# One matrix product of a delta-rule loop is moved behind two others in the order of the matrix engine

## What is computed

```python
def step(St, inp):
    q_i, k_i, u_i, kcd_i, dec_i, g_i = inp
    attn = jnp.einsum('bhid,bhjd->bhij', q_i, k_i) * dec_i
    v_new = u_i - jnp.einsum('bhid,bhdv->bhiv', kcd_i, St)
    inter = jnp.einsum('bhid,bhdv->bhiv', q_i * jnp.exp(g_i)[..., None], St)
    out_i = inter + jnp.einsum('bhij,bhjv->bhiv', attn, v_new)
    g_last = g_i[..., -1]
    St_new = St * jnp.exp(g_last)[..., None, None] + jnp.einsum('bhid,bhiv->bhdv', k_i * jnp.exp(g_last[..., None] - g_i)[..., None], v_new)
    return (St_new, out_i)
```

## Time and profile before

| | |
|---|---|
| median of 3 runs | 3433.17 us |
| lowest, highest | 3423.48, 3434.26 us |
| the profiled execution's own time | 3425.84 us |
| its span, first to last instruction | 3424.1 us |
| PE busy | 3096.7 us (90%) |
| PE's weight loads busy | 2439.5 us (71%) |
| DVE, ACT, POOL busy | 69%, 57%, 55% |
| mean granted clock of TensorE | 0.936 |

### The profile page before, as it was taken

The page is one execution under the profiler, slowest core; times in us unless marked ns, Lnnn a source line. Parts: engine busy times, 40 slices in busy tenths (PEclk is TensorE's granted clock), DMA queues, the critical chain, the costliest instruction groups (busy, mean ns, idle before and its releaser), DMA issues. The chain is left out here.

```text
span 3424.1 us, 150774 instructions
## 1 busy us (share of the span) xinstructions
PE 3096.7 (90%) x57344; PEld 2439.5 (71%) x57344; DVE 2362.8 (69%) x5828; ACT 1954.4 (57%) x5384; POOL 1866.6 (55%) x3982
## 2 busy tenths in 40 slices
PE   3599999999999999999999999999999999945880
PEld 2477777777777777777777777777777777722660
DVE  2377777777777777777777777777777777775114
ACT  2366666666666666666666666666666666630000
POOL 1265555555555555555555555555555555522773
PEclk8699999999999999999999999999999999976555
DMA  9201010111000000101111011010101010103555
GB/s 120 51 19 28 17 31 18 28 21 28 21 25 20 28 21 25 25 25 23 22 24 24 25 18 31 18 28 16 31 18 31 18 31 18 31 1 84 131 116 127
DMA packets 113784, 121.25 MB, mean 35 GB/s; under 512 B 17140, under 2 KB 105684, under 8 KB 113236
## 3 DMA queue, kind: packets, MB, share of 16 engines
q1 hardware_dynamic: 107608, 113.78, 15.2%
q0 software_dynamic: 6144, 7.09, 1.4%
HBM read 103.00 MB, written 17.01 MB: 35 GB/s over the span
## 5 line engine op out<-in xcount | busy, mean ns | idle before, releaser
L863 DVE SCALAR_TENSOR_TENSOR conv<-raw,conv_w,conv 128x256 f32<-128x256 f32 x1560 | 775.8, 504 | 447.4 <-ACT conv L741 410.3
L1096 POOL TENSOR_TENSOR core_ms<-core_ss,q_scale 128x2 f32<-128x2 f32 x256 | 74.9, 293 | 1028.8 <-ACT squares L794 1028.8
L498 PE MATMUL bank<-xT,w_proj 128*128 (+1 forms) x2080 | 564.9, 395 | 43.6 <-DMA w_proj<-in_w_proj 43.6
L781 ACT COPY rounds<-pair_bank 128x768 f32<-128x768 f32 x516 | 409.5, 794 | 245.8 <-PE pair_bank L577 245.8
L915 DVE TENSOR_TENSOR plus_one<-rounds,ident_half 128x256 f32<-128x256 f32 x774 | 411.0, 531 | 196.9 <-ACT rounds L781 186.7
L577 PE MATMUL pair_bank<-rounds 64*64 64x64 f32 x18576 | 457.4, 225 | 3.0 <-ACT rounds L781 3.0
L577 PEld LDWEIGHTS pair_bank<-rounds 64*64 64x64 f32 x18576 | 371.2, 134 | 111.3 <-issue 111.3
L498 PEld LDWEIGHTS bank<-xT,w_proj 128*128 128x128 f32 x2080 | 356.9, 191 | 103.1 <-issue 66.1
L768 ACT ACTIVATE vb<-bank,v_scale 128x128 f32<-128x128 f32 x516 | 162.1, 370 | 439.6 <-PE bank L529 439.6
L577 PE MATMUL pair_bank<-rounds,plus_one 64*64 64x64 f32 x10320 | 282.9, 221 | 23.0 <-DVE plus_one L915 5.3
L648 PE MATMUL bank<-w_out,gated 128*128 128x256 f32 x1024 | 285.7, 401 | 8.8
(11 more groups left out here) (275 smaller groups left out, 6598.7 us busy)
## 6 DMA issues: line engine op xcount, KB each, us to landing
e_blk<-e_rows SPq DMA_DIRECT2D x260, 128.0 KB, 4.0
g_blk<-g_rows SPq DMA_DIRECT2D x262, 64.0 KB, 3.4
w_gate_up<-in_w_gate_up SPq DMA_DIRECT2D x64, 192.0 KB, 2.8
w_proj<-in_w_proj SPq DMA_DIRECT2D x17, 512.0 KB, 4.0
table<-zeros_wide SPq DMA_DIRECT2D x32, 262.0 KB, 9.5
part<-table SPq DMA_DIRECT2D x32, 256.0 KB, 9.7
w_down<-in_w_down SPq DMA_DIRECT2D x16, 384.0 KB, 5.4
w_z<-in_w_proj SPq DMA_DIRECT2D x17, 256.0 KB, 3.1
```

Of the source, the lines that this page charges most:

```text
L498: mm = te.matmul(bank[bk][:, place * 2 * BLK:(place + 1) * 2 * BLK], w, k.xT[:, kt, bass.ds(rr * 2, 2)].rearrange("p c b i -> p b c i"), s ...
L781: a.copy(rounds[:, i % 2].rearrange("p b s w x -> p b (s w x)"), pair_bank[:, :, 0:6 * C]).then_inc(s["ul_out"], 1)
L863: v.scalar_tensor_tensor(out=conv[:, t], in0=raw[:, t, :, w:w + BLK], scalar=conv_w[:, t, w:w + 1], in1=conv[:, t], op0=ALU.mult, op1=ALU. ...
```

## The change

`project_out(st, n)` goes from ahead of `grow(st + 1, ...)` to behind `sum_squares(n + 2)`. Nothing is added or left out, and the orders of the other engines stay.

```diff
                 attend(st + 1, n, slot + 1)
                 a_round(m, 5)
-                project_out(st, n)
                 grow(st + 1, n, slot + 1)
                 sum_squares(n + 2)
+                project_out(st, n)
                 project(rr1, Z_ + 1, 0, 1, "projected_z")
                 turn_core(st + 1, m)
                 a_round(m, 6)
```

## The result

The changed kernel takes 3497.49 us (median of 4 runs, 3488.66 to 3498.46) against 3432.28 us before (4 runs, 3423.48 to 3434.26). The ratio is 1.0189, with a 95% interval of 1.0165 to 1.0214. So it is slower by 65 us; 59 were forecast.

A forecast was written before the change was run, and what follows sets the result against it. PE's order was taken to bound the loop. A stall of 0.68 us at the sums of squares, net 0.46 a body over 128 bodies, adds 59 us to 3429.2: forecast 3488 us, range 3466 to 3516.

The forecast's parts named there:

- The delay at the release: At the sums of squares: time from the end of ACT's square until PE goes on, taken as 0.12 us.
- step 5: Gate's projection on PE: behind the output projection instead of quarter-array work it is 0.10 us shorter, 0.87 for 0.97.
- 0.04 behind such an end: On DVE: `add_y` starts 0.04 us behind the output projection's modelled end, at 1504.44.
- what the queue swallows: At the transposes' weight load on PE: a possible 0.06 us lateness from `add_y`, taken as 0.
- the 0.46 of the sum: End of each body: `turn_core` at 1505.11 against 1504.65, 0.46 us later; 128 bodies give 59 us.
- Rival 2: On DVE: `add_one` still takes 1.00 us, making a body 0.83 longer, +106 us, 3535 us; chance 0.05.
- Rival 1: At the sums of squares: the square isn't late, PE needn't stand still, 28 us gained, 3401 us; chance 0.07.
- the 28 us: On PE: without any wait `turn_core` starts 0.22 us earlier in each body, 28 us in all.
- The lower bound of the range: No delay at the release: 0.34 us a body, +44 us, counted from the lowest run, 3467 us.

The follow-up runs named there:

- its control: The kernel before, with the sums of squares taken of the same constant tile so PE has no wait for ACT's square: 3428.86 us, ratio 0.9989.

## Why the prediction was right, point by point

**The mechanism** is the one forecast. The sums of squares were covered by the output projection; without that cover PE stands and waits for ACT. The wait is 0.66 in the timeline (0.68 forecast), it grows to 1.19 with the sums still earlier, and the loss goes with it in two kernels that remove it by different means.

**The terms**, on the clock of the earlier trace rows: growth 0.32 behind round 5's last part (0.36), sums at 1502.25 (1502.24), output projection at 1503.28 (1503.27), gate's projection at 1504.25 (1504.24). The delay at the release was bounded by 0 and 0.24 and taken as 0.12; it is 0.13, 1509.64 to 1509.77. The gate's projection is 1.03 long, not 1.13, as step 5 had it.

**The term that was mis-sized** is the start of `add_y`, "0.04 behind such an end". By the rows above, the projection's modelled end is 1510.80 + 1.13 = 1511.93 and `add_y` starts at 1512.12, so 0.19 behind. Less 7.52, it ends at 1505.02 (1504.86 forecast), and the weights of the transposes load at 1505.13:

```profile
1512.65 0.20 PEld L641 LDWEIGHTS bank<-ident,core_n 128*128 128x128 f32 x2 [0.26 <-issue]
```

That is 0.21 behind where they would have loaded unhindered (1504.92), past what the queue swallows: the transposes are 0.05 late, the gate 0.08 (1505.61 for 1505.53), and with that the body shown. Over the 128 bodies the mean is 0.50 more than before, for the 0.46 of the sum: 64 us for 59.

No run took this delay away by itself, but the trace of the changed kernel has bodies without it. In six blocks of each pair of heads `add_y` takes the place of its sum from a loop's counter; in the last two, which stand behind that loop in the code, the place is a constant. In these 32 bodies `add_y` starts 0.04 behind the projection's modelled end, in the other 96 it starts 0.16 to 0.18 behind (0.19 by the rounded rows above). One of the 32, on PE and DVE:

```profile
1577.73 1.10 PE L511 MATMUL bank<-ones_col,sq 128*64 128x1 f32 x32 [0.66 <-ACT sq L751]
1578.76 1.13 PE L648 MATMUL bank<-w_out,gated 128*128 128x256 f32 x4
...
1580.59 0.38 PE L641 MATMUL bank<-ident,core_n 128*128 128x128 f32 x2
```

```profile
1579.93 0.42 DVE L951 TENSOR_TENSOR y_sum<-bank,y_sum 128x256 f32<-128x256 f32 x1 [0.76 <-PE bank L648]
```

The transposes start 2.86 behind the sums (2.87 forecast, 1502.24 to 1505.11), and these bodies are 22.57 or 22.58 long; 22.57 was forecast. The others are 22.63 to 22.70. In the kernel before, both kinds are 22.10 to 22.15. So the 0.46 is right where the 0.04 holds, and the mis-sized term costs some 0.07 in three bodies of four.

The trace of before had the right figure. The second `add_y` of each body waits there for its projection:

```profile
1505.70 1.10 PE L648 MATMUL bank<-w_out,gated 128*128 128x256 f32 x4
```

```profile
1506.97 0.42 DVE L951 TENSOR_TENSOR y_sum<-bank,y_sum 128x256 f32 x1
```

It starts 0.17 behind the modelled end (1506.80). The prediction took its 0.04 from ACT's copy, another instruction.

**Rival 2** fell as argued: `add_one` behind the end of `state_d` takes 0.41.

**Rival 1** was rightly held unlikely, but its price was wrong. I gave it all of the 28 us if the square weren't late; without the wait it is 10 against its control. The prediction followed PE's own distances there and didn't ask what the transposes, round 6 and the gate would wait for next: `core_n`, done at 1504.41 on the old clock, and `add_one` beside `state_d`, both visible in the trace of before:

```profile
1503.78 0.63 ACT L800 ACTIVATE core_n<-bank,core_f 128x128 f32<-128x128 f32 x2 [1.12 <-POOL core_f L1104]
```

Even in the old order the weights of the transposes load 0.05 behind that end (1504.46), in all 128 bodies; so without a faster `core_n` they could come at most 0.19 earlier. As for the rule of the Trainium skill that stood beside this rival, on the change of the tiling mode (TensorEngine Tiling (Array Packing), section "Key Properties"), the trace agrees: with two mode changes fewer PE's distances are shorter, the output projection's 0.97 for 1.06. Most of it is lost to those waits.

**The reference point.** The forecast started from the mean of the four executions, 3429.2; the medians differ by 65.2, and the loop by 63.3. The lower bound of the range comes to 3467 by its own terms, and 3466 was stated.

## What to carry to other kernels

Before a call is moved out of an engine's order, subtract its length from the slack of every call that it stood in front of: here the sums had 0.53 to spare behind ACT's square, and the call taken away was over a microsecond long. A gain from a better order on the busiest engine is only worth what the next waits leave of it; go through the operands of the following calls and see when each is ready. Read what a wait costs from rows of the very instruction that will wait: here the second `add_y` already showed 0.17 where 0.04 was taken from another. A producer that is late for its new place can, as here, be moved to an engine's idle time, and that, with the order, is one change and not two.

## What the runs showed of the hardware that was not expected

Doubling the wait didn't only double its cost. With 1.19 of idle time in each body the granted clock fell in every third body, just behind the wait, and that body was 1.58 longer; with 0.66 in each body (the changed kernel) the loop kept a granted clock of 1.00:

```profile
300.00:1500.00 1200.00, 1153.15 (x23124) 928.26 (x23117) 855.25 (x2274) 772.89 (x2122) 679.96 (x1537) 1.00 0.10 23
```

```profile
L951 DVEq FUSED_REGOPS  x192: 75/75/93, 176.8 to 3008.5; - x192
```

So a register instruction of 0.08 to 0.09 us comes with the counter, and with it the later start. That is a comparison of bodies within one trace; no run changed the one thing alone.
